# Combining routed expert rows: a scatter that adds in DRAM in place of loading and adding two rows per token

## What is computed

```python
x = x + tanh(g_xattn[0]) * xattn(layernorm(x), ctx, ...)      # 16 heads, 64 context rows
xf = layernorm(x)                                             # 2048 tokens x 256
sh = gelu(xf @ sw1 + sb1)                                     # S = 2 shared experts, 512 hidden
shared_out = (sum_s sh @ sw2 + sb2.sum(0)) / S
gates = xf @ router_w + router_b                              # E = 8
topv, topi = top_k(gates, 2);  probs = softmax(topv)
comb = sum_k one_hot(topi_k) * probs_k                        # n x E
y = gelu(xf @ w1[e] + b1[e]) @ w2[e] + b2[e]
x = x + tanh(g_ffn[0]) * (shared_out + sum_e comb[:, e] * y[e])
```

## Time and profile before

| | |
|---|---|
| time, median of 3 runs | 427.12 us (426.74 to 428.44) |
| profiled execution, first to last instruction | 431.7 us (no other time is given for it) |
| PE busy | 393.3 us (91%) |
| DVE busy | 289.7 us (67%) |
| ACT busy | 252.9 us (59%) |
| POOL busy | 216.0 us (50%) |
| mean granted clock of PE | 0.972 of full speed |
| DMA | 42.66 MB, mean 99 GB/s |

### The profile page before, as it was taken

How to read it: one execution, slowest core, us unless ns; L and a number is a source line. 1 busy time by engine, 2 the same in 40 slices (tenths; PEclk the granted TensorE clock), 3 DMA queues, 4 the chain that set the end, 5 groups by cost and what they waited for, 6 DMA issues and landing times.

```text
span 431.7 us, 9073 instructions
## 1 busy us (share of the span) xinstructions
PE 393.3 (91%) x2720; PEld 363.5 (84%) x2721; DVE 289.7 (67%) x623; ACT 252.9 (59%) x614; POOL 216.0 (50%) x242
## 2 busy tenths in 40 slices
PE   3989999999999988989797788999999999999945
PEld 2878789999999888988696777999999999999945
DVE  3379788889899954896373787555555555553797
ACT  1356464757576466465556376667776776667421
POOL 6226667688887655478688240222222222223490
PEclk9999999999999998999979699999999999999997
DMA  7999400000000007329622011222222222211844
GB/s 205 292 332 298 97 2 2 1 2 2 0 0 0 2 2 255 135 66 314 219 88 98 0 38 49 75 76 73 73 84 76 73 84 74 73 61 50 281 158 146
DMA packets 33303, 42.66 MB, mean 99 GB/s; under 512 B 3026, under 2 KB 27548, under 8 KB 33276
## 3 DMA queue, kind: packets, MB, share of 16 engines
q1 hardware_dynamic: 28972, 32.17, 25.0%
q0 software_dynamic: 3408, 9.33, 6.2%
q10 hardware_dynamic: 896, 0.81, 0.6%
HBM read 25.75 MB, written 16.55 MB: 98 GB/s over the span
## 4 chain that ended last, share of the span: by engine, by line
PE 66%; DVE 14%; ACT 5%; DMA 4%; issue 4%; another core or an unknown queue 3%; POOL 2%; SPq 0%; DVEq 0%; ACTq 0%; POOLq 0%
PE psum L1134 12%; PE psum L1121 12%; PE psum L961 8%; PE psum L983 8%; PE psum L1019 4%; PE psum L1050 4%; PE psum L1152 4%; DVE xs_all L1555 3%; PE psum L867 2%; PE psum L939 2%; DMA wk_sb<-in_L_xattn_Wk 2%; PE psum L1110 2%; PE psum L902 2%; DMA y_got<-y_tok 1%
## 5 line engine op out<-in xcount | busy, mean ns | idle before, releaser
L602 POOL DMA_INDIRECT y_tok<-ysl,dest x39 | 37.5, 961 | 103.3 <-ACT ysl L812 103.3
L1529 DVE COPY hs<-psum 128x512 f32<-128x512 f32 x39 | 26.9, 691 | 52.8 <-issue 45.3
L828 ACT ACTIVATE hr<-psum,b_cur 128x128 f32<-128x128 f32 x156 | 44.5, 368 | 5.8 <-PE psum L1152 2.6
L592 POOL DMA_INDIRECT x_slot<-y_all,pos x32 | 35.9, 1121 | 10.5 <-issue 9.1
L746 ACT ACTIVATE early_stage<-psum,vec_col 128x256 f32<-128x256 f32 x48 | 20.0, 469 | 34.0 <-PE psum L1019 26.9
L549 POOL TENSOR_TENSOR Eb<-Eb,rinv 128x512 f32<-128x512 f32 x32 | 33.6, 1068 | 7.1 <-DVE rinv L1295 7.1
L812 ACT ACTIVATE ysl<-psum 128x256 f32<-128x256 f32 x39 | 14.9, 383 | 37.5 <-PE psum L1121 37.5
L533 POOL TENSOR_TENSOR half_sum<-Eb 128x512 f32<-128x512 f32 x16 | 20.6, 1288 | 20.9 <-ACT Eb L693 20.9
L721 ACT ACTIVATE yTb<-psum 128x256 f32<-128x256 f32 x16 | 6.2, 384 | 42.1 <-PE psum L1002 42.1
L1050 PE MATMUL psum<-sw_hi,early_hT_hi 128*128 128x256 f32 x96 | 26.7, 305 | 3.5 <-issue 2.8
L1134 PE MATMUL psum<-w_hi,xsT_hi 128*128 x78 | 27.9, 439 | 0.5 <-DVE xsT_lo L1513 0.5
(11 more groups left out here) (221 smaller groups left out, 1220.1 us busy)
## 6 DMA issues: line engine op xcount, KB each, us to landing
w_raw<-in_L_ffn_w SPq DMA_DIRECT2D x2, 4096.0 KB, 13.5
x_slot<-zero_row SPq DMA_DIRECT2D x1, 5011.5 KB, 21.7
xsl<-x_slot SPq DMA_DIRECT2D x39, 128.5 KB
y_got<-y_tok SPq DMA_DIRECT2D x8, 512.0 KB, 8.6
xs_all<-in_x SPq DMA_DIRECT2D x4, 512.0 KB, 14.9
sw_raw<-in_L_ffn_sw SPq DMA_DIRECT2D x2, 1024.0 KB, 12.5
out<-xs_all SPq DMA_DIRECT2D x5, 256.0 KB, 2.1
wq_sb<-in_L_xattn_Wq SPq DMA_DIRECT2D x2, 512.0 KB, 6.6
```

Source lines behind the costliest of these rows:

```text
L592: nc.gpsimd.indirect_dma_start(x_slot, bass.IndirectOffsetOnAxis(ap=pos[:, k, t:t + 1], axis=0), y_all[:, t, :], None).then_inc(scattered, 16)
L602: nc.gpsimd.indirect_dma_start(y_tok, bass.IndirectOffsetOnAxis(ap=dest[:, s:s + 1], axis=0), ysl[:, s % 2, :], None).then_inc(y_stored[s ...
L828: last = nc.scalar.activation(hr[:, m, :], bank[4 + par][:, m * P:(m + 1) * P], ACT.Gelu, bias=b1_cur[:, par, m:m + 1])
L1529: nc.vector.tensor_copy(hs[:, :], bank[2 + par][:, :]).then_inc(h_ready, 1)
```

## The change

1. A row of `x_slot` gets E = 8 more words, the token's weight for each expert (0 where it isn't chosen). The address word is now the token's row for both choices, so the wait between the two passes of row scatters goes. The softmax moves ahead of the counting on DVE, and Exp ahead of chunk 1 on ACT.
2. In each step DVE copies the weight of the tile's expert from `xsl` to one of four columns of `w_cur`, and ACT's copy to `ysl` multiplies by it.
3. SP stores the rows of `xs_all` to `y_acc` in DRAM as a base: tiles 12 to 15 (without their shared part) and 0 to 9 at once, 10 and 11 when chunk 5 is added. These three DMAs stand between the second and the third load of `xsl`.
4. The scatter adds onto `y_acc` (compute_op ADD). The two rows of a token may now stand in neighbouring slot tiles, so each scatter waits until the one before has landed.
5. At the end SP loads tiles 12 to 15 to `y_late` and copies tiles 0 to 11 from `y_acc` to `out`, DRAM to DRAM, 1.5 MB. DVE adds chunks 6 and 7 onto `y_late` (`add_last`), which are stored tile by tile. `y_got`, `add_routed`, `routed_pair`, `store` and POOL's part of the combining go.

```diff
-ROW = D + 1
-GROUP_OUT = 4
+ROW = D + 1 + E
+IN_RING = 4
...
-        y_tok = nc.dram_tensor("y_tok", [TOPK * TOK + SLOTS, D], F32, kind="Internal").ap()
+        y_acc = nc.dram_tensor("y_acc", [TOK + SLOTS, D], F32, kind="Internal").ap()
...
+        BASE = ((0, (EARLY - 1) * TPS), ((EARLY - 1) * TPS, EARLY * TPS))
+        EARLY_ROWS = EARLY * TPS * P
...
+            def keep_base(first, end):
+
+                sp.dma_start(y_acc_tiles[:, first:end, :], xs_all[:, first:end, :]).then_inc(base_stored, 16)
+
+            keep_base(EARLY * TPS, NT)
+            for first, end in BASE:
+                sp.wait_ge(acc_free, end + 2)
+                keep_base(first, end)
+
...
-            for g in range(NT // GROUP_OUT):
-                tiles = slice(g * GROUP_OUT, (g + 1) * GROUP_OUT)
-                for k in range(TOPK):
-                    sp.dma_start(y_got[:, k, tiles, :], y_tok_tiles[:, k, tiles, :]).then_inc(y_loaded[g], 16)
-
-
-            for n, pair in enumerate(VECTOR_PAIRS):
-                store(sp, pair, 1, n)
-            sp.wait_ge(out_stored, 16 * NT // TPS)
+            sp.dma_start(y_late[:, :, :], y_acc_tiles[:, EARLY * TPS:NT, :]).then_inc(late_loaded, 16)
+            sp.dma_start(out_flat[0:EARLY_ROWS, :].rearrange("(a n) d -> a (n d)", a=P),
+                         y_acc[0:EARLY_ROWS, :].rearrange("(a n) d -> a (n d)", a=P)).then_inc(out_stored, 16)
+
+
+            for t in range(EARLY * TPS, NT):
+                sp.wait_ge(out_ready, t - EARLY * TPS + 1)
+                sp.dma_start(out_rows[:, t, :], xs_all[:, t, :]).then_inc(out_stored, 16)
+            sp.wait_ge(out_stored, 16 * (1 + NT - EARLY * TPS))
...
+            pool.wait_ge(names_ready, 1)
+            pool.wait_ge(weights_kept, 1)
             for k in range(TOPK):
-                if k:
-                    pool.wait_ge(scattered, 16 * NT)
-                    name_rows(k)
-                pool.wait_ge(names_ready, k + 1)
                 for t in range(NT):
                     nc.gpsimd.indirect_dma_start(x_slot, bass.IndirectOffsetOnAxis(ap=pos[:, k, t:t + 1], axis=0),
                                                  y_all[:, t, :], None).then_inc(scattered, 16)
...
+            pool.wait_ge(base_stored, 16 * (1 + len(BASE)))
             for s in range(SLOT_TILES):
                 pool.wait_ge(ye_ready, s + 1)
-                nc.gpsimd.indirect_dma_start(y_tok, bass.IndirectOffsetOnAxis(ap=dest[:, s:s + 1], axis=0),
-                                             ysl[:, s % 2, :], None).then_inc(y_stored[s % 2], 16)
-
...
+                if s:
+                    pool.wait_ge(y_stored[(s - 1) % 2], 16 * ((s + 1) // 2))
+                nc.gpsimd.indirect_dma_start(y_acc, bass.IndirectOffsetOnAxis(ap=dest[:, s:s + 1], axis=0),
+                                             ysl[:, s % 2, :], None, compute_op=ALU.add).then_inc(y_stored[s % 2], 16)
...
-            shared(1, early)
-            columns(2, early)
-
             act.wait_ge(dif_ready, 1)
             nc.scalar.activation(ex[:, :], dif[:, :], ACT.Exp).then_inc(ex_ready, 1)
             warm_gelu()
+            shared(1, early)
+            columns(2, early)
...
-                nc.scalar.activation(ysl[:, par, :], bank[6 + par][:, 0:D], ACT.Copy).then_inc(ye_ready, 1)
-
-            def step(s, par, *_):
+                nc.scalar.activation(ysl[:, par, :], bank[6 + par][:, 0:D], ACT.Identity,
+                                     scale=w_cur[:, ring:ring + 1]).then_inc(ye_ready, 1)
...
+            dve.wait_ge(ex_ready, 1)
+            link(nc.vector.tensor_scalar(den[:, :], ex[:, :], 1.0, None, ALU.add))
+            link(nc.vector.reciprocal(prob[:, 0, :], den[:, :]))
+            link(nc.vector.tensor_tensor(prob[:, 1, :], ex[:, :], prob[:, 0, :], ALU.mult))
+            for k in range(TOPK):
+                link(nc.vector.tensor_tensor(ohp[:, k, :, :], oh[:, k, :, :],
+                                             prob[:, k, :].unsqueeze(2).broadcast_to([P, NT, E]), ALU.mult))
+            link(nc.vector.tensor_tensor(place[:, :, :], ohp[:, 0, :, :], ohp[:, 1, :, :], ALU.add))
+            nc.vector.tensor_scalar(y_all[:, :, D + 1:], place[:, :, :], tg[:, 1:2], None, ALU.mult
+                                    ).then_inc(weights_kept, 1)
+            link(nc.vector.memset(comb[:, :, :], 1.0))
+            link(nc.vector.tensor_scalar(comb[:, :, 0:E], place[:, :, :], float(S), None, ALU.mult))
             for t in range(TPS):
                 add_shared(0, t, acc_free)
...
-            link(nc.vector.tensor_copy(emap[:, :], emap_f[:, :]))
-
-            dve.wait_ge(ex_ready, 1)
-            link(nc.vector.tensor_scalar(den[:, :], ex[:, :], 1.0, None, ALU.add))
...
-            link(nc.vector.memset(comb[:, :, :], 1.0))
-            link(nc.vector.tensor_tensor(place[:, :, :], ohp[:, 0, :, :], ohp[:, 1, :, :], ALU.add))
-            nc.vector.tensor_scalar(comb[:, :, 0:E], place[:, :, :], float(S), None, ALU.mult).then_inc(routed_all, 1)
+            nc.vector.tensor_copy(emap[:, :], emap_f[:, :]).then_inc(routed_all, 1)
+
             dve.wait_ge(routed_all, 1)
...
-                nc.vector.tensor_tensor(dest[:, at(s)], xsl[:, par, D:].bitcast(I32), spare[:, at(s)], ALU.min)
+                ring = u % IN_RING
+                nc.vector.tensor_tensor(dest[:, at(s)], xsl[:, par, D:D + 1].bitcast(I32), spare[:, at(s)], ALU.min)
+                nc.vector.tensor_copy(w_cur[:, ring:ring + 1], xsl[:, par, bass.ds(expert(u) + (D + 1), 1)])
                 nc.vector.tensor_tensor(xsT_lo[:, :, :], bank[par][:, 0:D].rearrange("p (k n) -> p k n", k=KD),
                                         xsT_hi[:, :, :].bitcast(F32), ALU.subtract).then_inc(xt_lo, 1)
...
-            def add_routed(pair, done):
...
-                        nc.vector.scalar_tensor_tensor(row, y_got[:, k, t, :], wgt[:, k, t:t + 1], row, ALU.mult, ALU.add
...
+            def add_last(c):
+
+                if c == EARLY:
+                    dve.wait_ge(late_loaded, 16)
+                for t in range(TPS):
+                    dve.wait_ge(acc_psum, c * TPS + (t + 1))
+                    nc.vector.scalar_tensor_tensor(xs_all[:, c * TPS + t, :], bank[6 + t][:, 0:D], half_tg[:, 0:1],
+                                                   y_late[:, (c - EARLY) * TPS + t, :], ALU.mult, ALU.add)\
+                        .then_inc(out_ready, 1)
+                if c < LAST:
+                    dve.wait_ge(out_ready, (c - EARLY + 1) * TPS)
+                    dve.sem_inc(acc_free, TPS)
+
+            for c in range(EARLY, NSUB):
...
+                if c < LAST:
+                    bias_weights(c + 1)
+                    columns_rest(c + 1, late)
+                add_last(c)
```

More of the change, by code:

```diff
@@ L184, in build @@
         late = shared_buffers("late", AT_W + W_WORDS, AT_W + W_WORDS + 2 * KD * SUB)
-        y_got = at_words("y_got", [P, TOPK, NT, D], AT_W)
-        assert TOPK * NT * D <= W_WORDS and 2 * KD * SUB + 4 * SUB + 2 * HT_WORDS <= W_WORDS
+        y_late = at_words("y_late", [P, NT - EARLY * TPS, D], AT_W)
+        assert (NT - EARLY * TPS) * D <= W_WORDS and 2 * KD * SUB + 4 * SUB + 2 * HT_WORDS <= W_WORDS
         (xsl, xsT_hi, xsT_lo, hs, hr, hr_hi, hr_lo, ysl), end = row_of(AT_STEP, [
@@ L269, in build @@
         y_stored = [sem(f"y_stored{i}") for i in range(2)]
[L270 to L274, removed]
+        base_stored, late_loaded, bias_psum = sem("base_stored"), sem("late_loaded"), sem("bias_psum")
+        out_ready, out_stored = sem("out_ready"), sem("out_stored")
         x_rows = x.rearrange("b (t p) d -> p (b t) d", p=P)
@@ L278, in build @@
         x_slot_tiles = x_slot.rearrange("(s p) d -> s p d", p=P)
-        y_tok_tiles = y_tok[0:TOPK * TOK, :].rearrange("(k t p) d -> p k t d", k=TOPK, p=P)
+        y_acc_tiles = y_acc[0:TOK, :].rearrange("(t p) d -> p t d", p=P)
+        out_flat = out.rearrange("b t d -> (b t) d")
         block = st.enter_context(nc.Block())
@@ L369, in routed @@
                 step(s, s % 2, s)
-        PAIRS_OUT = NT // TPS
-        POOL_PAIRS = (0, 2, 4)
-        VECTOR_PAIRS = [pair for pair in range(PAIRS_OUT) if pair not in POOL_PAIRS]
         LAST = NSUB - 1
[L378 to L390, removed]
+        BASE = ((0, (EARLY - 1) * TPS), ((EARLY - 1) * TPS, EARLY * TPS))
+        EARLY_ROWS = EARLY * TPS * P
         def tiles_before(s, par):
@@ L489, in _ @@
             nc.gpsimd.iota(iota_slot_i[:, :], [[1, SLOT_TILES]], base=0, channel_multiplier=0).then_inc(counters, 1)
-            nc.gpsimd.iota(spare[:, :], [[P, SLOT_TILES]], base=TOPK * TOK, channel_multiplier=1).then_inc(counters, 1)
+            nc.gpsimd.iota(spare[:, :], [[P, SLOT_TILES]], base=TOK, channel_multiplier=1).then_inc(counters, 1)
             nc.gpsimd.memset(comb_cur[:, :, :], 0.0).then_inc(counters, 1)
             nc.gpsimd.memset(zero_row[:, 0:D], 0.0).then_inc(zeros_ready, 1)
```

(17 more changed lines are left out.)

57 lines of the change are left out of this document (9 added, 48 removed).

## The result

| | before | after |
|---|---|---|
| median of 5 runs | 428.44 us (426.74 to 437.2) | 459.42 us (457.32 to 472.95) |
| ratio, 95% interval | | 1.0735 (1.0667 to 1.0804) |
| profiled execution, span | 431.7 us | 469.7 us |

The change makes the kernel 7% slower; forecast were 418 us and, as the range, 416 to 446. In this document medians are of all runs, while ratios and intervals are of the undisturbed ones only: two of the five of after, the profiled one (span 469.7 us) and one of 471.0, took about 13 us longer than the other three (455.3 to 457.6). In the profiled one the loss lies between 198 and 231 us, ahead of the routed loop. From the first scatter on the trace can be read as it stands.

What follows compares the result with a forecast made beforehand. The prediction took the tail to be bound by combining routed rows on DVE and POOL. Its sum was 431.7 - 9.7 + 1.0 - 0.6 = 422.4 us span, 417.8 in the median's terms, called 418; range 416 to 446.

Steps and rivals of the forecast that it cites:

- the cycle: Routed loop: time from one scatter's start to the next when each waits for the previous landing; taken as 3.5 us.
- the crossing at 3.57: Scatter-to-scatter time in us at which the scatters' end, 283.0 + 39C, overtakes the 422.4 us end of the hidden case.
- The 0.81 us for DMA: Routed loop, each scatter: 0.38 us for a second stream of 128 KB plus 0.43 us for reading DRAM.
- The end formula: Kernel end if scatters pace it: 283.0 + 39C, C being the scatter-to-scatter time, including 15.4 us after the last landing.
- Rival (a): Routed loop: serial scatters become the bound and cost more than the tail gives, from 3.81 us each; chance 0.35.
- the chain hidden: Routed loop: serial scatters stay within PE's 3.47 us step, so the span is 422.4 us; chance 0.42.
- The tail: After the loop: the 4 MB load, 20 DVE adds and 9 POOL operations go; 9.7 us less.
- DVE's new copy: Routed loop: one 128x1 weight copy per step, free within 0.5 us of slack; without that cover 0.2 us x 37.
- Rival (d): Routed loop: ACT's scaled copy needs table loads, 5.0 us a step, some 55 us more; chance 2 in 100.
- base stores' 1.0 us: Routed block's start: stores ahead of the third `xsl` load make PE 1.0 us late, bounds 0 and 2.
- The routing's -0.6 us: Routing before the loop: DVE's block gets 0.6 us shorter after operations move or go, bounds -1.5 and +1.5.
- The bound from above, 4.7: Routed loop: upper limit in us for a serial adding scatter, reading the rows as a separate 2.0 us DMA first.

Runs made afterwards that it cites:

- plain serial: The changed kernel with plain-write scatters (nothing added in DRAM), each still waiting for the one before: 425.58 us median, ratio 0.9909 to the kernel before.
- halved widths: The changed kernel scattering only 128 of 256 numbers of each row, still in series: adding, 437.3 us; with plain scatters, span 418.8 us (one run each).
- kernel without the wait: The changed kernel with each scatter adding onto spare rows of its own, not waiting for the one before: 421.08 us median, ratio 0.9808 to the kernel before.
- other three ratios: Changed kernel with plain scatters still waiting, 0.9909; with adding scatters alternating between two tables, 0.9862; with plain scatters into two planes, 0.9921.

## Why the prediction was wrong

**The step that failed** is the cycle, "2.68 + 0.38 + 0.43 = 3.49 us, and I take 3.5": it measures 4.52. Term by term:

| term | taken | measured | from |
|---|---|---|---|
| landing to POOL's next start | 0.28 | 0.75 | plain serial: 3.15 - 2.4 |
| POOL's part of a scatter | 0.96 | 1.55 | tile `ysl` after |
| DMA behind POOL's part | 1.44 + 0.81 | 2.25 | 3.8 - 1.55 |
| sum | 3.49 | 4.55 | 4.52 seen |

The 0.28 came from a row where ACT released POOL; a landing releases it 0.47 us later. That is a mistake of kind: the change replaces a wait on an engine by a wait on a DMA, and I priced it by the engine's row. The 0.96 was taken although the text itself says that it "assumes POOL's 0.96 unchanged"; it priced "half again" with 4.0 and then did not take it. Each of these terms alone would have moved the forecast from the crossing at 3.57 to a loss.

**The 0.81 us for DMA is right as a sum and wrong in its parts.** I counted a second stream of bytes and a delay of 0.43 us for reading DRAM. The halved widths show, from single runs, three times the time by the byte (1.2 to 1.3 us against 0.4), and no added delay; that the sum agrees is luck. By the Trainium skill (DMA: Bandwidth & Descriptors, Anatomy of one DMA), three streams would have made a cycle near 3.2, an estimate; the plain scatters agree with its slope (0.15 us for 64 KB by it, 0.2 measured), but the measured cycle is 4.52, and the measurement decides.

**The end formula held.** 283.0 + 39C gives 459.3 at C = 4.52; the three shorter spans are 455.3 to 457.6. From the landing of the last scatter to the end I took 15.4 us (the terms listed add up to 15.5; nothing hangs on it); 450.9 + 3.8 = 454.7 to 469.7 are 15.0. The formula's sensitivity of 3.9 us for 0.1 us also holds: the 0.51 us that half the width takes from the cycle, times 39, is 20; the spans differ by 20 to 22. Rival (a) is what happened, beyond its price at 4.3 and within the one at 4.7.

**The rest of the sum.** With the chain hidden I forecast 422.4, that is 9.3 us or 2.2% less. The kernel without the wait is the changed one with its chain hidden; its interval, 1.5 to 2.4% less, holds that. The other three ratios say 0.8 to 1.4% less.

The tail was right. From the start of the last copy to `ysl` to the end of the span are 35.3 us before and 25.3 or 25.4 in the four kernels with the changed tail and a hidden chain: 10.0 less, for the 9.7 forecast. PE's products of chunk 7 do run without the wait for `bias_w`.

What the sum lacks is the loop. I called DVE's new copy free because `xsT_lo` had 0.5 us of slack. One step of the kernel before and then one of the plain serial kernel:

```profile
332.07 0.42 DVE L1513 TENSOR_TENSOR xsT_lo<-psum,xsT_hi 128x256 fp32r<-128x256 f32 x1
332.97 0.71 PE L1134 MATMUL psum<-w_hi,xsT_hi 128*128 x2
```

```profile
332.50 0.41 DVE L1492 TENSOR_TENSOR xsT_lo<-psum,xsT_hi 128x256 fp32r<-128x256 f32 x1
333.07 0.72 PE L1109 MATMUL psum<-w_hi,xsT_hi 128*128 x2
```

The slack has shrunk from 0.48 to 0.16 us, and PE starts 0.09 us later behind its previous work, which the profile doesn't count as idle. In the middle of the loop the step is 3.55 or 3.56 us in all six kernels that weight the rows and hide the chain, against 3.47 and 3.48 in the two that don't weight them. From the first to the last copy to `ysl` that makes 132.1 to 132.4 us against 129.6 and 129.9: some 2.5 us that I had put at nothing. DVE's copy (0.15 us) and ACT's scaled copy (0.47 us where the unscaled took 0.38) are both new in the step; no run separates them. Beside the 39 x 1.0 us of the chain this is small, but it is a quarter of what the tail gives.

Rival (d) fell: no table is loaded in the loop. Of the base stores' 1.0 us (bounds 0 and 2) the traces show this much: from the second to the third `xsl` tile that PE turns are 4.9 to 6.2 us in the seven kernels with all three stores, 4.9 in the one with weighted rows but without them, and 4.7 before. The routing's -0.6 us is below what these runs can tell; neither term was tested by itself.

**Chances.** I gave the loss 0.37, of which 0.35 to rival (a), and let the range end at C = 4.3. The bound from above, 4.7, was the nearer one, though for another reason: it adds a read of 2.0 us of its own, where the excess over 2.68 is 0.47 + 0.59 + 0.81 us of three kinds. The point estimate sat 0.07 us below a crossing with a slope of 3.9 us for each 0.1 us, with a term, POOL's 0.96, that its own text calls assumed; that is where the likeliest case should have changed sides.

## What to carry to other kernels

An operation that updates the same memory again and again forms a serial chain: compare its whole cycle (issue, transfer, and the release after a landing) with the step that has to hide it, and price each link by a row of the same kind. If it does not fit, split the target so that neighbours are independent; the second table costs zeros stored ahead, one more read and some wide additions, here 0.6 us of tail (25.9 against 25.3). And where a small term is multiplied by the number of steps, take its pessimistic value into the forecast when the crossing is near.

## What the runs showed of the hardware

- An accumulating indirect scatter of 128 rows x 1 KB keeps POOL for 1.55 us, the plain one for 0.96. With half the width both stay; with half the rows they are 1.41 and 0.90 (single runs).
- It lands after 3.8 us against 2.4, and by single runs its bytes take about three times as long. It leaves three times the packets on the queue, 144 against 48: from 300 to 380 us 23 scatters leave 3312 without the wait, and 1104 in the kernel before. With half the width they are still 144 (2880 for 20).
- POOL starts a scatter 0.73 to 0.75 us after a landing that it waits for, and 0.28 us after an engine's instruction; ACT starts 0.02 us after the same landing.
- Adding scatters onto two tables, the last of them landing after 3.7 us, did not slow PE's loop, at a DMA share of 0.47: the step is 3.55 us, and 3.56 with plain scatters into two planes.
